# Attention pass of a graph network: the one-hot matrix is held still, and the sums are lifted back in a second step

## The reference, cut to what matters

```
def gat_conv(h, src, dst, W, att_src, att_dst, gat_b, n):
    xh = (h @ W).reshape(n, H, C)                       # H = 4 heads, C = 32
    a_src = jnp.einsum('nhc,hc->nh', xh, att_src)
    a_dst = jnp.einsum('nhc,hc->nh', xh, att_dst)
    alpha = jax.nn.leaky_relu(a_src[src] + a_dst[dst], NEG_SLOPE)
    amax = jax.ops.segment_max(alpha, dst, num_segments=n)
    alpha = jnp.exp(alpha - amax[dst])
    denom = jax.ops.segment_sum(alpha, dst, num_segments=n)
    alpha = alpha / denom[dst]
    msg = xh[src] * alpha[:, :, None]
    out = jax.ops.segment_sum(msg, dst, num_segments=n)
    return out.reshape(n, H * C) + gat_b
```

## Time and profile before

| | |
|---|---|
| time, median of 3 runs | 16186.12 us (16180.12 to 16220.35) |
| profiled execution, its time | 16321.94 us |
| its span | 16320.2 us |
| PE busy, share of the span | 7191.9 us, 44% |
| DVE busy | 3356.4 us, 21% |
| ACT busy | 1018.3 us, 6% |
| POOL busy | 9435.0 us, 58% |
| gathers of the attention pass (L1273) | 1568, first at 7367.2 us, last at 10581.5 us |
| span and granted TensorE clock | 0.545 of full speed |

### The profile page before, as it was taken

How to read it: one execution, slowest core, us unless ns; L and a number is a source line. 1 busy time by engine, 2 the same in 40 slices (tenths; PEclk the granted TensorE clock), 3 DMA queues, 4 the chain that set the end, 5 groups by cost and what they waited for, 6 DMA issues and landing times. The chain is left out here.

```text
span 16320.2 us, 114373 instructions
## 1 busy us (share of the span) xinstructions
PE 7191.9 (44%) x33118; PEld 6193.0 (38%) x33119; DVE 3356.4 (21%) x6077; ACT 1018.3 (6%) x1883; POOL 9435.0 (58%) x9490
## 2 busy tenths in 40 slices
PE   3333333333333444443544455585555556333333
PEld 2333333333332323323444444444555554333333
DVE  4222221010001111122222222243111113211111
ACT  1000000000000000000000000031000001100000
POOL 2666666666666666654444444404666663466666
PEclk8555555555555555555555555565555556555555
DMA  2111111111112222221111111113222222212112
GB/s 88 48 47 47 48 47 44 49 47 48 48 48 51 57 58 56 58 56 36 37 37 37 37 36 36 36 49 103 83 81 85 82 81 71 80 53 55 53 53 53
DMA packets 502661, 905.35 MB, mean 55 GB/s; under 512 B 171985, under 2 KB 324470, under 8 KB 500896
## 3 DMA queue, kind: packets, MB, share of 16 engines
q0 software_dynamic: 301056, 623.59, 15.1%
q1 hardware_dynamic: 201412, 279.27, 5.2%
HBM read 795.34 MB, written 106.87 MB: 55 GB/s over the span
## 5 line engine op out<-in xcount | busy, mean ns | idle before, releaser
L761 POOL DMA_INDIRECT work<-rows_a,index x4704 | 4676.8, 994 | 2318.8 <-issue 1546.0
L823 PE MATMUL psum<-onehot,work 128*128 128x80 f32 x12544 | 2706.8, 411 | 4543.6 <-DMA work<-rows_a,index 3108.6
L823 PEld LDWEIGHTS psum<-onehot,work 128*128 128x128 f32 x12544 | 2615.0, 320 | 4650.6 <-issue 4636.5
L761 POOL DMA_INDIRECT work<-rows_b,index x3136 | 3170.7, 1011 | 1667.8 <-issue 1067.0
L1273 POOL DMA_INDIRECT regionC<-attention_rows,index x1568 | 1541.1, 983 | 1765.4 <-PE psum L1356 1210.3
L905 DVE TENSOR_TENSOR regionA<-regionA,psum 128x80 f32 x980 | 230.6, 235 | 5310.2 <-remote 3475.0
L823 PE MATMUL psum<-onehot,regionB 128*128 128x80 f32 x3136 | 748.6, 410 | 713.2 <-issue 541.7
L823 PEld LDWEIGHTS psum<-onehot,regionB 128*128 128x128 f32 x3136 | 716.2, 327 | 740.4 <-issue 735.7
L834 PE MATMUL psum<-onehot,regionB 128*128 128x80 f32 x3136 | 751.4, 412 | 430.8 <-issue 430.6
L834 PEld LDWEIGHTS psum<-onehot,regionB 128*128 128x128 f32 x3136 | 716.5, 328 | 443.0 <-issue 442.7
L1392 PE MATMUL psum<-turn,work 128*128 128x16 f32 x1568 | 334.8, 305 | 1020.8 <-issue 1020.8
(11 more groups left out here) (321 smaller groups left out, 6866.3 us busy)
## 6 DMA issues: line engine op xcount, KB each, us to landing
regionB<-in_edge_attr SPq DMA_DIRECT2D x195, 512.0 KB
work<-rows_a,index POOLq DMA_INDIRECT x4704
work<-rows_b,index POOLq DMA_INDIRECT x3136
regionC<-attention_rows,index POOLq DMA_INDIRECT x1568
x_transposed<-regionA SPq DMA_DIRECT2D x75, 250.0 KB, 6.1
rows_a<-regionC SPq DMA_DIRECT2D x50, 250.0 KB
h_transposed<-regionB SPq DMA_DIRECT2D x50, 250.0 KB
regionB<-h_transposed SPq DMA_DIRECT2D x2, 6250.0 KB, 25.2
```

The source lines that it names most:

```text
L761: pool.indirect_dma_start(rows3[h][:, t, :], None, table, bass.IndirectOffsetOnAxis(ap=net.index[:, k, h * ST + t:h * ST + t + 1], axis=0) ...
L823: last = nc.tensor.matmul(bank_of(h, q, 0), msgs3[h][:, t, 0:D], onehot[:, h * ST + t, :], start=(k == 0), stop=(k == GT - 1))
```

## The change

The sums are formed the other way round. For each group, four matmuls hold the one-hot matrix still (128 edges by 64 nodes) and move the whole gathered row, 136 columns, features and weights together. That gives nodes by 136 numbers, in PSUM with two groups side by side on 64 partitions each and two after one another. ACT then copies the four groups of a half into two buffers (`hold`), and TensorE turns them back into features by nodes (`lift`): a transpose for the 128 features and a product with the identity for the 8 weights, twice. DVE adds from the lifted result in PSUM bank 5. To make room, the products of L1392 always use bank 4, and some small scratch fields move from region C to the end of region B. GpSimd now waits for `packed[1]`, raised by the sums, not for the lifted result.

```
-    past, coming = Cc[0:H, spare + 384:spare + 417], Cc[0:H, spare + 417:spare + 450]
...
+    tail = N + W4
+    past, coming = B[0:H, tail:tail + 33], B[0:H, tail + 33:tail + 66]
...
+    held = [Cc[:, spare + 384:spare + 384 + XW], net.wtmp[:, 3 * P:3 * P + XW]]
...
-                    pool.wait_ge(summed[1], n + 1)
+                    pool.wait_ge(packed[1], n + 1)
...
+                def hold(n, h):
+                    act.wait_ge(packed[h], n + (4 if h else 1))
+                    act.wait_ge(summed[1 - h], n + (2 if h else 1))
+                    for x in range(2):
+                        y = S.copy(held[x], bank(6 + h)[:, x * XW:(x + 1) * XW])
+                    y.then_inc(held_ready[h], 1)
...
+                    if not isinstance(j, int):
+                        hold(act.snap(n - 1), 0)
                     act.wait_ge(own_ready, n + 2)
                     act.wait_ge(scored, n + 2)
-                    S.copy(own_edge, bank(4 + k)[:, 0:256]).then_inc(own_copied, 1)
+                    S.copy(own_edge, bank(4)[:, 0:256]).then_inc(own_copied, 1)
...
                     S.activation(own_p, u[:, P:2 * P], ACT.Exp).then_inc(weighed, 1)
+                    if not isinstance(j, int):
+                        hold(act.snap(n - 1), 1)
...
-                    pe.wait_ge(added[h], n + 1)
+                    pe.wait_ge(held_ready[h], n + 1)
...
-                            T.matmul(bank(6 + h)[:, q * W4:(q + 1) * W4], ring[s][:, t, 0:D], onehot[k][:, t, :],
-                                     start=(i == 0), stop=(i == GT4 - 1))
-                        for i in range(GT4):
-                            t = h * HALF + q * GT4 + i
-                            m = T.matmul(bank(6 + h)[32:32 + 2 * H, 256 + q * W4:256 + (q + 1) * W4],
-                                         ring[s][:, t, D:XW], onehot[k][:, t, :],
+                            m = T.matmul(bank(6 + h)[q % 2 * W4:(q % 2 + 1) * W4, q // 2 * XW:(q // 2 + 1) * XW],
+                                         onehot[k][:, t, :], ring[s][:, t, :],
                                          start=(i == 0), stop=(i == GT4 - 1))
-                    m.then_inc(summed[h], 1)
+                    m.then_inc(packed[h], 1)
+
+                def lift(n, h):
+                    pe.wait_ge(held_ready[h], n + 2)
+                    pe.wait_ge(added[1 - h], n + (2 if h else 1))
+                    for x in range(2):
+                        T.transpose(bank(5)[:, x * P:(x + 1) * P], held[x][:, 0:D], net.ident[:, :])
+                        t = T.matmul(bank(5)[32:32 + 2 * H, 256 + x * P:256 + (x + 1) * P], held[x][:, D:XW],
+                                     net.ident[:, :], start=True, stop=True)
+                    t.then_inc(summed[h], 1)
...
+                    if not first:
+                        lift(pe.snap(n - 1), 0)
                     pe.wait_ge(flips_copied, n * 4 + 6)
-                    pe.wait_ge(own_copied, n + 1)
+                    pe.wait_ge(own_copied, n + 2)
...
                         sums_of(pe.snap(n - 1), (s + 2) % 3, 1 - k, 1)
+                        lift(pe.snap(n - 1), 1)
...
-                    dve.wait_ge(summed[h], n + (4 if h else 1))
+                    dve.wait_ge(summed[h], n + 2)
```

More of the change, by code:

```diff
@@ L1209, in gat_pass @@
     cross = Cc[:, spare + 320:spare + 384]
-    past, coming = Cc[0:H, spare + 384:spare + 417], Cc[0:H, spare + 417:spare + 450]
-    carried = Cc[0:H, spare + 450:spare + 514]
-    peaks, change, alpha = Cc[0:H, spare + 514:spare + 516], Cc[0:H, spare + 516:spare + 517], Cc[0:H, spare + 517:spare + 518]
-    first_own, final = Cc[0:H, spare + 518:spare + 520], Cc[0:H, spare + 520:spare + 521]
+    tail = N + W4
+    past, coming = B[0:H, tail:tail + 33], B[0:H, tail + 33:tail + 66]
+    carried = B[0:H, tail + 66:tail + 130]
+    peaks, change, alpha = B[0:H, tail + 130:tail + 132], B[0:H, tail + 132:tail + 133], B[0:H, tail + 133:tail + 134]
+    first_own, final = B[0:H, tail + 134:tail + 136], B[0:H, tail + 136:tail + 137]
+    held = [Cc[:, spare + 384:spare + 384 + XW], net.wtmp[:, 3 * P:3 * P + XW]]
     score_of = [net.turn[:, k * P:(k + 1) * P] for k in range(2)]
@@ L1217, in gat_pass @@
     flags = [net.rows[:, k * 2 * P:(k + 1) * 2 * P] for k in range(2)]
-    u, own_p = net.wtmp[:, 0:3 * P], net.wtmp[:, 3 * P:4 * P]
+    u, own_p = net.wtmp[:, 0:3 * P], net.wtmp[:, 2 * P:3 * P]
     u4 = u.rearrange("p (k t h) -> p k t h", k=3, h=H)
@@ L1248, in gat_pass @@
     message, summed, added = [[sem(f"{k}{h}") for h in range(2)] for k in ("message", "summed", "added")]
+    packed, held_ready = [[sem(f"{k}{h}") for h in range(2)] for k in ("packed", "held")]
     step, sums = sem("step"), sem("sums")
@@ L1302, in _ @@
             act.sem_inc(own_copied, 2)
+            for h in range(2):
+                act.sem_inc(held_ready[h], 1)
             R = act.value_load(net.rounds[0:1, 1:2], min_val=1, max_val=256)
@@ L1332, in turn @@
                     S.activation(own_p, u[:, P:2 * P], ACT.Exp).then_inc(weighed, 1)
+                    if not isinstance(j, int):
+                        hold(act.snap(n - 1), 1)
                 each(act, r, turn)
+                n = act.snap(r * NIT + (NIT - 1))
+                for h in range(2):
+                    hold(n, h)
         @block.tensor
@@ L1339, in _ @@
             pe.sem_inc(chained, 1)
-            pe.sem_inc(summed[1], 3)
+            pe.sem_inc(packed[1], 3)
+            for h in range(2):
+                pe.sem_inc(summed[h], 1)
             R = pe.value_load(net.rounds[0:1, 1:2], min_val=1, max_val=256)
@@ L1388, in turn @@
                              start=True, stop=True).then_inc(chained, 1)
+                    if not first:
+                        lift(pe.snap(n - 1), 0)
                     pe.wait_ge(flips_copied, n * 4 + 6)
-                    pe.wait_ge(own_copied, n + 1)
+                    pe.wait_ge(own_copied, n + 2)
                     for q in range(HALF):
-                        m = T.matmul(bank(4 + k)[:, q * 16:(q + 1) * 16], flipped[:, q * P:(q + 1) * P],
+                        m = T.matmul(bank(4)[:, q * 16:(q + 1) * 16], flipped[:, q * P:(q + 1) * P],
                                      blocks[:, q // 2 * 16:q // 2 * 16 + 16], start=True, stop=True)
@@ L1407, in _ @@
                     sums_of(n, (NIT - 1) % 3, (NIT - 1) % 2, h)
+                    lift(n, h)
         @block.vector
@@ L1420, in _ @@
             V.memset(B[32:64, :], 0.0)
-            V.memset(B[0:2 * H, N:REG], 0.0)
+            V.memset(B[0:2 * H, N:tail], 0.0)
             V.memset(den_select, 0.0)
@@ L1473, in add @@
                         counted(V.tensor_tensor(den[:, bass.ds(at[q], W4)], den[:, bass.ds(at[q], W4)],
-                                                bank(6 + h)[32:32 + 2 * H, 256 + q * W4:256 + (q + 1) * W4], ALU.add))
+                                                bank(5)[32:32 + 2 * H, 256 + q * W4:256 + (q + 1) * W4], ALU.add))
                         x = V.tensor_tensor(A[:, bass.ds(at[q], W4)], A[:, bass.ds(at[q], W4)],
-                                            bank(6 + h)[:, q * W4:(q + 1) * W4], ALU.add)
+                                            bank(5)[:, q * W4:(q + 1) * W4], ALU.add)
                         if q == GQ - 1:
```

## The result

| | before | after |
|---|---|---|
| median of 4 runs, us | 16,187.2 (16,180 to 16,220) | 15,609.9 (15,601 to 15,616) |
| ratio | | 0.9643 [0.9627, 0.9659] |
| span of the profiled execution, us | 16,320 | 15,602 |
| median turn of the attention pass, us | 66.6 | 54.6 |
| from the release to the next gather, us | 20.4 | 8.3 |

A forecast was written before the change was run, and what follows sets the result against it. Waits bound the attention pass: the way from a turn's last gather to the end of half 1's sums. 46 turns x 0.7 us = +32, with -12 elsewhere, gave +20 on 16,186: 16,206 us, range 15,990 to 16,290.

The forecast's parts named there:

- the release: Moment about 6 us after a turn's last gather when TensorE's queue, slow during gathers, is emptied at once.
- slow queue: What TensorE completes leaves through a queue draining slowly beside gathers; when full, PE slows, one load or move in 0.63 us.
- Step 1: Sums of half 1, on the path: 32 pairs at 0.227 us, 7.5 us instead of 11.4, gain 3.9 us a turn.
- Step 2: Sums of half 0, beside the gathers: 2 to 4 us shorter, buying nothing since what follows waits for the release.
- Step 3: Lift of half 0 ahead of L1392's products: if `packed[0]` comes only with the release, L1548 is 4.6 us later.
- the round trip: PE posts `packed[0]`, ACT copies, PE lifts: 0.6 us of copies plus 1.5 us of lift; bounds 1.5 to 3.1 us.
- B: Rival: half 0's signal gets out before the release; up to 3.9 us a turn gained, 15,995 us; chance 0.29.
- Steps 4 and 5: Lift and copies of half 1 under the gathers; moved scratch fields, bank 4 and one more memset range: both cost nothing.
- C: Rival: full clock for the sums of half 1, 4.0 instead of 7.5 us, 16,045 us; chance 0.07.
- S: Rival: load and move do not overlap, a half takes 10.9 us, 16,375 us; chance 0.14.

The follow-up runs named there:

- Half 0 alone: Against the kernel before: only half 0 in the new form (one-hot stationary, copies, lift), half 1 with its 64 old matmuls; 0.9842, -255 us, late chip.

## Why the prediction was wrong, step by step

- **What bounds the kernel.** Right: the way from the release to the end of half 1's sums set the turn; POOL's wait was the term that moved, and the reading of a slow queue that is emptied after the last gather stood up to half the gathers (release 3.9 us after the last) and to doubled sums. That holds for late chips; on prompt ones the gathers themselves set the turn.
- **Step 1, sums of half 1: mis-sized.** The pair at 0.227 us was right. The sum 32 x 0.227 = 7.3, with its tail 7.5, left out that consecutive groups write opposite columns and overlap: 4.98 us at the low clock, 2.5 less. The clock, which rose near the end of the half, took it to 4.45, another 0.5. The gain was 7.0 us a turn and not 3.9; the difference, 3.1 x 46 = 143 us.
- **Step 2, half 0 "buys nothing of itself": wrong.** Half the instructions there is what lets the signals out. Half 0 alone brought 255 us.
- **Step 3, the lift held until the release, +4.6 us: the step that failed.** `packed[0]` came 3.5 us late and not 30. Doubling the pairs of half 0 brings the forecast back exactly: release, lift, 32 pairs in 7.0 us, L1578 10.0 us after the release against the 9.8 worked out. So the price of the round trip was right and its condition was not. I had taken the 0.63 us for each load and move, measured behind 58 pairs of half 0, as the pace from near the start of the half on (B allowed for a faster start); the rows show that the first 55 to 59 pairs leave at full pace. The trace before showed it already: half 0 ran at full pace until 9491.21, and the new half 0 has 32 pairs in all.
- **Steps 4 and 5.** Right: nothing appeared there.
- **Rival B** had the mechanism (0.29), but its gain was capped at 3.9 us a turn, and a turn's chain and additions before the release, 5.1 us, were not in it: they replace the 4.6 that I had charged as a loss. With both sizes put right B gives -12.1 a turn. My objection to it, that signals stood still for over 20 us in every turn, spoke of signals behind twice as many instructions. **C** happened in small part: the granted clock was 0.58 over half 1, the last 0.7 us of it near full, worth some 0.5 us a turn and not 3.5. **S** did not: L1373's halves show overlap, not serial work.
- **The range** was bounded by B with my size of half 1. Both errors had one sign, and neither was in it.

## What to carry to other kernels

Where an engine's signals come late beside a stream of indirect gathers, count its instructions ahead of the signal, not its busy time: with 32 pairs ahead of it a signal came 3.5 us late, with 64 it came 29 us late. Here 32 pairs that write the two halves of the array cost 3.9 us alternated and 6.3 with one change of half, so look at the output partitions of neighbours before multiplying a pair's time by its count. And time a kernel on more than one chip before a wait's removal is booked as a gain: the same change was worth 3.6% on one and 0 to 0.2% on two others.

## What the runs showed of the hardware that I had not expected

- Chips seem to differ in whether GpSimd's gathers hold up TensorE's signals. The kernel before took 16,187, 16,274 and 16,287 us on the chip of the result, on 10 and on 1, and 14,074, 14,082 and 14,082 on 11, 13 and again 11, the runs of a series within some 0.3% of one another. Chip 11 was prompt both times, with 10, 13 and 1 measured in between; no late chip was measured twice, so that the kind belongs to the chip is likely and not shown. What differs is open: the traces of the changed kernel show the same instructions, the same 87 instruction fetches and the same pace of the gathers, 1.25 us in the median.
- TensorE gets 55 to 59 pairs of load and move off at full pace beside gathers, in the turns shown, before it slows to one in 0.7 to 2.6 us; some 70 where it waits for a copy among them.
- A gather that meets one of DVE's operations of 2,048 columns takes up to 3.0 us and not 0.94 and ends 0.8 us after it; this took back 65 and 89 us from two versions with a shorter wait.
- With 16 gathers instead of 32 the release follows the last one after 3.9 us and not 5.8 to 6.1. The number of gathers is not all that sets this: with half 1 put first it came 2.2 us after the last of 32.
